# Convolution stage with masks from bf16 sign products, folded pyramid weights and running sums; expert blocks stored by their number

## The reference

```python
# L0, over 8 steps of 2 images each, on the group-normalised x
u = 0.5 * u + xt;  s = (u > 1.0);  u = u - s          # s: spikes, 0 or 1
ch_att = conv1d(mean over pixels of s, w_channel)      # one number per image and channel
sp_att = conv2d([mean over channels, max over channels], w_spatial)   # one per image and pixel
tem    = conv1d(mean of everything per step, w_temporal)
mask   = (tem * ch_att * sp_att >= 0);  x = x + s * mask
# L1, on the group-normalised new x
y1, y2, y4 = means of x over the image, its quarters and its sixteenths, each laid out as 4 x 4
z = conv(conv([y1, y2, y4], w1), w2);  gate = sigmoid(fc2(relu(fc1(z))));  x = x + xn * gate
# L2 mixture: for each token the two best experts' outputs, weighted
```

## Time and profile before

| | us |
|---|---|
| median of 3 runs (lowest, highest) | 4566.6 (4561.16, 4569.98) |
| the profiled execution | 4562.08 |
| its span in the trace | 4560.4 |
| convolution stage, until the last engine has reached its end | 0 to 303 |
| attention stage, until the first mixture | 303 to 2390 |
| first mixture, decay stage, second mixture | 2390 to 4560 |

### The profile page before, as it was taken

The page is one execution under the profiler, slowest core; times in us unless marked ns, Lnnn a source line. Parts: engine busy times, 40 slices in busy tenths (PEclk is TensorE's granted clock), DMA queues, the critical chain, the costliest instruction groups (busy, mean ns, idle before and its releaser), DMA issues. The chain is left out here.

```text
span 4560.4 us, 74420 instructions
## 1 busy us (share of the span) xinstructions
PE 3719.4 (82%) x21802; PEld 1983.8 (44%) x21802; DVE 3278.3 (72%) x6678; ACT 2140.1 (47%) x3740; POOL 1924.8 (42%) x2046
## 2 busy tenths in 40 slices
PE   1627999989999898999947994488888786999999
PEld 0111222332333332333216883255555555777777
DVE  6737788888888888888815664555556566777777
ACT  1012666666666666666636773122222233444444
POOL 0311033322223323332234553466666653777776
PEclk9976999999999999999978997699999998999999
DMA  2982111121122222222003331000000001000000
GB/s 74 353 302 39 24 30 35 30 37 32 34 36 37 38 37 38 37 37 37 11 23 121 105 105 53 16 30 29 28 28 28 28 19 33 24 23 23 23 23 23
DMA packets 132977, 237.52 MB, mean 52 GB/s; under 512 B 27632, under 2 KB 32952, under 8 KB 132600
## 3 DMA queue, kind: packets, MB, share of 16 engines
q1 hardware_dynamic: 115736, 200.51, 16.4%
q0 software_dynamic: 16384, 33.59, 2.5%
q10 hardware_dynamic: 576, 0.02, 0.0%
HBM read 89.74 MB, written 144.31 MB: 51 GB/s over the span
## 5 line engine op out<-in xcount | busy, mean ns | idle before, releaser
L1143 ACT ACTIVATE b_probs<-b_ps_s 128x512 f32<-128x512 f32 x2048 | 1173.8, 596 | 708.1 <-PE b_ps_s L1187 670.0
L940 DVE TENSOR_REDUCE b_maxes<-b_ps_m 128x1 f32<-128x1024 f32 x1024 | 1215.6, 1214 | 268.7 <-PE b_ps_m L1175 266.0
L1187 PE MATMUL b_ps_s<-b_qs,b_ks 99*128 99x512 bf16 x2048 | 788.9, 390 | 54.8 <-DMA b_ks<-b_k_parts 15.2
L1175 PE MATMUL b_ps_m<-b_ks,b_qs 96*128 96x512 bf16 x2048 | 642.5, 396 | 113.5 <-DVE b_maxes L940 92.0
L1881 POOL TENSOR_TENSOR e_act_lo<-e_act,e_act_hi 128x512 fp32r<-128x512 f32 x384 | 521.8, 1359 | 239.4 <-DVE e_act_hi L1810 239.4
L1199 PE MATMUL b_ps_o<-b_probs,b_vs 128*32 128x512 f32 x4096 | 559.6, 619 | 23.6 <-ACT b_probs L1143 22.8
L1187 PEld LDWEIGHTS b_ps_s<-b_qs,b_ks 99*128 99x128 bf16 x2048 | 199.3, 98 | 845.6 <-ACT b_probs L1143 668.8
L2082 ACT ACTIVATE e_act<-e_ps_h,e_bias 128x512 f32<-128x512 f32 x384 | 264.3, 689 | 411.6 <-PE e_ps_h L2136 290.9
L1985 DVE TENSOR_TENSOR e_act<-e_act,e_ps_g 128x512 f32<-128x512 f32 x384 | 261.5, 681 | 145.9 <-ACT e_act L2082 145.9
L814 POOL TENSOR_TENSOR b_rstd<-b_mv,b_eps 128x8 f32<-128x8 f32 x32 | 6.5, 202 | 744.5 <-DVE b_mv L921 744.5
L1175 PEld LDWEIGHTS b_ps_m<-b_ks,b_qs 96*128 96x128 bf16 x2048 | 188.7, 100 | 301.5 <-DVE b_maxes L940 179.3
(11 more groups left out here) (434 smaller groups left out, 7415.9 us busy)
## 6 DMA issues: line engine op xcount, KB each, us to landing
slots_out<-nothing SPq DMA_DIRECT2D x17, 4096.0 KB, 29.8
b_qs<-b_q_parts SPq DMA_DIRECT2D x96, 256.0 KB, 9.1
c_xin<-slots_in SPq DMA_DIRECT2D x71, 256.0 KB, 2.6
slots_out<-c_y_out SPq DMA_DIRECT2D x71, 256.0 KB, 2.0
b_q_parts<-b_qparts SPq DMA_DIRECT2D x16, 768.0 KB, 3.6
a_x<-in_x_dram SPq DMA_DIRECT2D x8, 1024.0 KB, 10.2
normalised_t<-d_xT SPq DMA_DIRECT2D x16, 512.0 KB
e_xb<-normalised_t SPq DMA_DIRECT2D x32, 256.0 KB, 2.8
```

The source lines that it names most:

```text
L940: nc.vector.tensor_reduce(maxes[:, kv, u:u + 1], ps_m[:, u % 2], AX.X, ALU.max).then_inc(m_free, 1)
L1143: nc.scalar.activation(probs[:, s % PROBS, j * HALF:(j + 1) * HALF], ps_s[:, j % 2], ACT.Exp).then_inc(exp_done, 1)
L1175: last = nc.tensor.matmul(ps_m[:, u % 2, half * HALF:(half + 1) * HALF], qs[0:STACK, buffer, h * PX + qt * P:h * PX + qt * P + P], ks[0:ST ...
L1187: nc.tensor.matmul(ps_s[:, j % 2], ks[0:rows, parity, kv * PX + tt * P:kv * PX + tt * P + P], qs[0:rows, parity, h * PX + half * HALF:h * ...
```

## The change

1. The band matrices are built after the first statistics; the spatial one is cut into three bf16 parts by POOL, and the 5 fp32 products become 15 bf16 ones.
2. In the 8 steps the compare covers both images in one instruction without the count, and one instruction forms `(u > 1) - u` (with the sign of the next factor turned). ACT counts the spikes, except in the last step.
3. The mask comes from signs. A pixel is kept when 3 * spike + sign(factor) * sign(row attention) (with signs turned, so that the sum is at least 2.5) is large enough. PE forms that sum per image with four bf16 products; the row signs go once more through DRAM. DVE compares and adds to `x` in one instruction. POOL has no part in it.
4. After each image DVE takes its 16 cell sums, and ACT its sum of squares. The two convolutions are folded into 16 weights per channel beforehand.
5. `slots_out` holds 71 blocks, block `j` at row `512 * j`. The 17 clearing transfers are gone. DVE turns `route["slots"]` into the new numbers in blocks 8 to 16 of the experts' stage.

```diff
@@ convolution_stage, SP
-            for k in range(FILLS):
-                sp.dma_start(slots_out[k * some:(k + 1) * some]..., nothing[:]...).then_inc(cleared, 16)
+            sp.wait_ge(row_signs_done, 1)
+            sp.dma_start(sign_dram.rearrange("i (y x) -> y i x", x=SIDE),
+                         row_signs[:].rearrange("y (i x) -> y i x", x=SIDE)).then_inc(signs_out, 16)
+            sp.wait_ge(signs_out, 16)
+            sp.dma_start(sign_maps[0:IMAGES], sign_dram).then_inc(signs_in, 16)
@@ DVE, the eight steps
-                    nc.vector.scalar_tensor_tensor(u[:], u[:], 0.5, xh[:, t % 2], ALU.mult, ALU.add
+                    nc.vector.scalar_tensor_tensor(u[:], u[:], -0.5, xh[:, t % 2], ALU.mult, ALU.add
...
+                if t < TIME - 1:
+                    nc.vector.tensor_scalar(spikes[:, t * PER_STEP * PX:(t + 1) * PER_STEP * PX], u[:],
+                                            1.0, None, ALU.is_gt).then_inc(spiked, 1)
+                    link(nc.vector.scalar_tensor_tensor(u[:], u[:], 1.0, u[:], ALU.is_gt, ALU.subtract))
@@ DVE, masks and sums
+            def add_kept(i):
+                dve.wait_ge(masked, i + 1)
+                xs = X[:, i * PX:(i + 1) * PX]
+                nc.vector.scalar_tensor_tensor(xs, ps_big[:, i % 2].rearrange("c h x -> c (h x)"), 2.5, xs,
+                                               ALU.is_ge, ALU.add).then_inc(x_added, 1)
+            def cell_sums(i):
+                dve.wait_ge(x_added, i + 1)
+                cells = X[:, i * PX:(i + 1) * PX].rearrange("c (b y x e) -> c b x y e", b=4, y=8, x=4)
+                return nc.vector.tensor_reduce(y4s[:, i].rearrange("c (b x) -> c b x", b=4), cells, AX.XY, ALU.add)
+            add_kept(0)
+            for i in range(1, IMAGES):
+                add_kept(i)
+                cell_sums(i - 1)
@@ ACT
+            for i in range(IMAGES):
+                act.wait_ge(x_added, i + 1)
...
+                nc.scalar.activation(junk[:, i % 2], X[:, i * PX:(i + 1) * PX], ACT.Square,
+                                     accum_out=squares[:, i:i + 1]).then_inc(squared, 1)
@@ PE
+            for i in range(IMAGES):
+                if i >= 2:
+                    pe.wait_ge(x_added, i - 1)
+                for h in range(2):
+                    at = i * PX + h * HALF
+                    nc.tensor.matmul(ps_big[:, i % 2, h], three[:], spikes[:, at:at + HALF], start=True, stop=False)
+                    last = nc.tensor.matmul(ps_big[:, i % 2, h], sign_diag[:, i], sign_maps[:, h * HALF:(h + 1) * HALF],
+                                            start=False, stop=True)
+                last.then_inc(masked, 1)
@@ experts_stage, SP
-                    at = sp.value_load(row_i[0:1, done:done + 1], min_val=0, max_val=SLOT_ROWS - SLOTS)
-                    sp.dma_start(slot_rows(slots_out, at), y_out[:, done % 2]).then_inc(y_sent[done % 2], 16)
+                    sp.dma_start(slot_rows(slots_out, done * SLOTS), y_out[:, done % 2]).then_inc(y_sent[done % 2], 16)
@@ experts_stage, DVE
+            def move_from(e):
+                renumber(nc.vector.scalar_tensor_tensor(
+                    beyond, route["slots"][:], float(e * REGION),
+                    jump[:, e:e + 1].broadcast_to([P, IMAGES * 2 * TILES]), ALU.is_ge, ALU.mult))
+                renumber(tt(placed, placed, beyond, ALU.add))
...
                 multiply(j, 0)
+                if j == E:
+                    block_starts()
+                if E < j < 2 * E:
+                    move_from(j - E)
+                if j == 2 * E:
+                    nc.vector.tensor_copy(route["slots"][:], placed)
```

More of the change, by code:

```diff
@@ L103, in convolution_stage @@
         average = sb("a_average", [P, IMAGES])
+        squares = sb("a_squares", [P, IMAGES])
+        junk = sb("a_junk", [P, 2, PX], BF16)
         picks = sb("a_picks", [P, 63], BF16)
[L105 to L106 removed]
+        maps = sb("a_maps", [2 * IMAGES, 2, HALF], BF16)
+        rows = sb("a_rows", [2 * SIDE, IMAGES, SIDE + TAPS - 1], BF16)
         ones = sb("a_ones", [P, TAPS, P])
@@ L250, in _, with inverse_root @@
             made(pool.memset(mean_all[:], 1.0 / C))
-            for norm in range(2):
+            made(pool.memset(sign_maps[:], 0.0))
+            made(pool.memset(sign_diag[:], 0.0))
+            made(pool.memset(taps[:], 0.0))
+            made(nc.gpsimd.tensor_scalar(three[:], ident[:], 3.0, None, ALU.mult))
+            def inverse_root(norm):
                 pool.wait_ge(variance, norm + 1)
@@ new lines, in _ @@
+            nc.vector.tensor_scalar(both[:, 0], tmp[:], 1.0 / PX, None, ALU.mult)
+            dve.wait_ge(squared, IMAGES)
+            nc.vector.tensor_scalar(both[:, 1], squares[:], 1.0 / PX, None, ALU.mult).then_inc(moments, 1)
+            group_moments(1)
+            link(nc.vector.tensor_tensor(
+                weighed[:], y4s[:],
+                folded[:].rearrange("p (a y) x -> p a (y x)", a=1).broadcast_to([P, IMAGES, 16]), ALU.mult))
+            link(nc.vector.tensor_reduce(raw[:], weighed[:], AX.X, ALU.add))
```

312 lines of the change are left out of this document (161 added, 151 removed).

## The result

| | us | predicted |
|---|---|---|
| kernel before, median of 4 runs (lowest, highest) | 4568.29 (4561.16, 4576.64) | |
| changed kernel, median of 4 runs (lowest, highest) | 4434.65 (4429.75, 4442.82) | 4438, 4425 to 4460 |
| ratio | 0.9706, 95% interval 0.9689 to 0.9724 | 0.9715 |
| first statistics of the attention stage | 183.83, before 316.90 | 185.5 |
| experts' blocks, first to last `multiply` | 360.9, before 357.6 | +5 |

The profiled execution of the changed kernel took 4442.82 us (span 4440.9) and is the slowest of its four. The two spans therefore differ by only 119.5, and I read the stages, not the span. A link is a wait of DVE for an instruction of its own.

The account below looks back on a forecast made before the run. Two things were taken to end the convolution stage: the compute chain at 289.8 and the clearing zeros at about 316. -131.4 at attention's start and +5 for experts give 4435.7 from 4562.08; with half of 4.5 added, 4438 us, range 4425 to 4460.

Parts of the forecast that it names:

- Statistics: Convolution stage's start: DVE's last statistic at 27.7, first step at 37.8; channel band at nothing, in DVE's wait for POOL.
- Steps: The convolution stage's eight steps on DVE: 5.93 us for one, 45.2 for all instead of 53.0.
- Rival B: In the steps, the new compare stays at one element a cycle, 2.3 instead of 1.23: 4446 us, chance 0.08.
- Signs: From the steps' end to the first mask: products, signs through DRAM and PE's first four products take 21.8 us.
- Pass: Masks, cell sums and squares in one pass: 2.46 us per image on DVE, 39.4 in all.
- rival A: In the mask pass, the cell sums run at the strided rate, 11 us more: 4449 us, chance 0.13.
- Tail: From the end of the mask pass to the gate network: 6.2 us; then scaling and turning x, 29.36.
- Boundary: Entry of the attention stage: first load after 1.3, first statistics 4.4 later, at 185.5 instead of 316.90: -131.4.
- Rival C: At the attention stage's entry, zeros were not what made weights slow; boundary keeps 11.2 (+7): 4445 us, chance 0.15.
- Experts: Experts' stage: renumbering lengthens the ring of DVE and ACT by 0.65 in blocks 9 to 15; +5 carried.
- Rival D: In the experts' stage, the new DVE instructions wait beside POOL, 0.45 more per block: 4442 us, chance 0.2.
- Rivals E and F: E: attention stage left at 1.2 GHz clock, 4640, chance 0.02; F: it still waits on SP, near 4470, chance 0.01.

Follow-up runs that it names:

- a_boundary2: Changed kernel with attention's first statistics not waiting for loads and constants, POOL setting `b_ks` behind the third parts, PE waiting for it only before its first reader: 4442.53 us.
- a_renumber_twice: Changed kernel with a second pair of DVE instructions that changes nothing behind each of the seven renumbering pairs in the experts' stage: 4447.77 us in one execution.
- a_again: The changed kernel once more, nothing altered: 4441.37 us, ratio 0.9728 to the kernel before.
- the two single ones: Kernel before without its 17 clearing transfers, with everything else of the change outside its convolution stage: 4552.63 us; changed kernel with those transfers put back: 4551.39 us.
- a_sums_apart: Changed kernel with all 16 cell sums behind the pass of compare-and-adds instead of one image behind each: 4447.95 us, ratio 0.9736 to the kernel before.

## Why the prediction was right

The time (4434.65 against 4438) and the place of the gain came out as forecast. That the sum is so close is in part luck: of the steps up to the attention stage's first statistics four came out shorter than forecast, by 4.3 us together, and three longer, by 2.7. Three of the signs named in the prediction did not come: the images are 2.26 apart (2.4 to 2.5), the attention stage's statistics follow the first load by 6.0 (within 5), and blocks 9 to 15 are 0.31 longer (0.6 to 1.1). By its own steps, the numbers after the colon being predicted and measured:

1. **Statistics**: last statistic 27.7, 28.10; first step 37.8, 38.78. Of the 1.0, 0.4 is the statistics' end and 0.8 POOL's first instruction, which took 1.02 us beside DVE's channel band (0.22 in the kernel before); the spatial band took 2.7 instead of 3.0. "At nothing" was too kind: both ran together and one paid.
2. **Steps**: 45.2, 44.7 for all, 5.93, 5.79 for one. The compare is 1.23 as chosen; DVE starts the next instruction 0.09 before the last one's end where no link stands between, which I had not counted. Rival B is out.
3. **Signs**: 21.8, 20.95. The way through DRAM took 98.95 to 102.49, 3.5 instead of 4.2. The rows of 64 bytes cost nothing visible: 1.73 out and 1.81 in, where the 64 KB of the maps, in rows of 1 KB, took 1.63 out (86.77 to 88.40). The price that the Trainium skill's rule ("DMA: Bandwidth & Descriptors", Specifications) would put at the upper end did not appear at 32 KB.
4. **Pass**: 39.4, 36.7. The instructions are 1.21 each, as worked out, but two pairs of them overlap by 0.08, so an image takes 2.26 and not 2.46. I had added 0.04 for links, which is not there either, since the add that a cell sum waits for lies three instructions back. The sum runs at the contiguous rate (1207 ns for 1024), so rival A is out: runs of 8 are as good as one long run.
5. **Tail**: 6.2, 6.28; scaling and turning 29.36, 29.38.
6. **Boundary**: last copy to first load 1.3, 1.0; first load to first statistics 4.4, 6.0. Rival C is out, since the loads issue in 0.36 to 1.22. But the step "what is late next" failed: I asked only for the loads' landing, and POOL's constants (5.9 us, `b_ks` 3.51 of them) were later. They stood in the earlier trace rows, as POOL's 5.67 us between 289.77 and 316.90, hidden under the zeros. a_boundary2 shows that the wait was worth 6.
7. **Experts**: +5, +3.3. The model of the ring was wrong. I took the 5.09 of a block as filled by DVE and ACT but for 0.29, from DVE's gaps. By itself the ring needs 4.5, and PE, the one engine that never pauses in the normal blocks, holds them at 5.09. The slack is 0.6, so a pair costs 0.31 and not 0.65; the second, as a_renumber_twice shows, costs 0.92. Smaller errors stood against this. Block 8 cost 1.17 (6.26), where I had 0.65. The buffers gave back 0.65, where I had 1: block 16 takes 4.69 and block 17 4.84. And 0.8 of the 3.3 lies in blocks without renumbering, where I expected no change. Rival D was seen once (1.00 instead of 0.17 at 2338.00, beside POOL) and not in the pairs.

The sum by these rows is -133.1 + 3.3 = -129.8, against the predicted -126.4: 4432.3. The profiled execution lies 10.5 above that, in the stages that the change does not touch: +6.5 in the attention stage and +3.7 at the end, stretches that differ by as much between profiles of kernels that are alike there; how far this is shown to be chance stands at a_again. Rivals E and F are out: the granted clock rose 103 to 109 us after the attention stage's first statistics in all these profiles, 102.6 in the kernel before, and the stage's first statistics are released by POOL and not by anything on SP.

The argument that bore the forecast, that only both parts together bring it, is shown by the two single ones: 14 and 15 us, against 125.

## What to carry to other kernels

When two things end a stage, price each alone and both together: here 20, 21 and 133 us. Removing either alone would have looked like a failure. When the last wait of a boundary goes, list everything that was hidden under it on every engine, not the next one on the same queue. Put bookkeeping into a wait that exists (DVE's 9.27 us for weights), and judge 3 us by its own stretch when executions of one kernel differ by 15 to 20.

## What the runs showed of the hardware that I had not expected

- The same 64x160 cast on POOL took 0.31 us beside a DVE compare with a count and 2.26 beside DVE's `(u > 1) - u` on 2048 elements. A cheaper DVE form can be dearer for its neighbour.
- An accumulated result costs a second instruction: 0.19 us on ACT (16 in the pass, 3.0 us in all) and 0.08 on DVE.
- PE's bf16 products of 512 columns took 0.63 us and from the third image on 0.38 in a_sums_apart, while its granted clock reads 1.00 over the whole stretch from 104.50 to 124.00. For such short stretches the duration in the rows is the surer reading.
